# Token rows scattered into slot order in the image loop, and plain loads of 128 rows per expert tile

## What is computed

```python
def reference(x, ...):
    h = tokens(x)                        # (16, 256, 192)
    h = h + attention(layernorm(h))      # 12 heads of 16, then a layernorm with gain and bias
    h = h + ffn(layernorm(h))
    return h

def ffn(x):
    probs = softmax(x @ Wr.T)            # 16 experts
    top_p, top_idx = top_k(probs, 2)
    for e in range(16):
        y += gate[e] * (gelu(x @ W1[e] + b1[e]) @ W2[e] + b2[e])   # gate is 0 where e isn't chosen
    return x + y
```

## Time and profile before

| | us |
|---|---|
| median of 3 runs | 898.73 (895.57 to 900.16) |
| profiled execution, its time | 903.53 |
| its span, first to last instruction | 901.7 |
| TensorE busy (matmul) | 741.2 (82%) |
| VectorE, ScalarE, GpSimd busy | 362.6, 355.0, 432.4 |
| mean granted TensorE clock | 0.907 of 2.4 GHz |

### The profile page before, as it was taken

One profiled execution on the slowest core, in us unless ns is written; L12 is line 12 of the kernel. 1 busy time (PEld: TensorE's weight loads), 2 busy tenths in 40 slices (PEclk: granted clock), 3 DMA queues, 4 the chain that ended last, 5 costly groups with the idle time before them and its releaser, 6 DMA issues.

```text
span 901.7 us, 18009 instructions
## 1 busy us (share of the span) xinstructions
PE 741.2 (82%) x5773; PEld 625.9 (69%) x5773; DVE 362.6 (40%) x984; ACT 355.0 (39%) x857; POOL 432.4 (48%) x618
## 2 busy tenths in 40 slices
PE   0776899967998989897842599999999999999950
PEld 0664567755776766675531499999999999999950
DVE  3101567844676857685453111111111111111128
ACT  0222376643565756564410133333333333333310
POOL 6751234644666756675674244444444443444310
PEclk9995699987999999998855699999999999999985
DMA  7614455576566576664101693726598777686239
GB/s 192 119 43 87 90 116 115 95 93 69 82 115 90 112 86 113 96 119 69 26 25 39 198 326 96 221 82 194 180 315 276 219 222 226 216 260 196 52 104 333
DMA packets 117477, 128.66 MB, mean 143 GB/s; under 512 B 23911, under 2 KB 102008, under 8 KB 117346
## 3 DMA queue, kind: packets, MB, share of 16 engines
q1 hardware_dynamic: 105906, 106.97, 49.1%
q0 software_dynamic: 11504, 20.85, 7.6%
HBM read 145.45 MB, written 29.89 MB: 194 GB/s over the span
## 4 chain that ended last, share of the span: by engine, by line
PE 69%; DMA 13%; DVE 6%; SPq 5%; issue 3%; ACT 2%; POOL 1%; DVEq 0%; ACTq 0%; POOLq 0%
PE BK L419 17%; PE BK L404 12%; PE BK L409 8%; DMA shared<-qk_parts 6%; PE BK L774 4%; PE BK L689 4%; PE BK L794 4%; PE BK L815 4%; PE BK L394 3%; DMA shared<-nmT 3%; PE BK L854 3%; PE BK L826 2%; DVE hr L525 2%; SPq L614 2%; PE BK L782 2%
## 5 line engine op out<-in xcount | busy, mean ns | idle before, releaser
L440 ACT ACTIVATE pixels<-BK,b1t 128x128 f32<-128x128 f32 x474 | 130.7, 375 | 222.0 <-PE BK L409 222.0
L553 POOL DMA_INDIRECT pair_rows<-shared x79 | 77.7, 983 | 190.4 <-DVE shared L507 186.6
L419 PE MATMUL BK<-shared,pixels 128*128 128x192 f32 x948 | 167.9, 326 | 0.3 <-ACT pixels L440 0.3
L419 PEld LDWEIGHTS BK<-shared,pixels 128*128 128x128 f32 x948 | 153.0, 190 | 0.7 <-ACT pixels L440 0.6
L1227 DVE TENSOR_REDUCE negmax<-BK 128x6 f32<-128x1536 f32 x64 | 112.5, 1758 | 34.9 <-PE BK L794 33.6
L404 PE MATMUL BK<-shared 128*128 128x128 f32 x948 | 120.0, 277 | 0.0
L404 PEld LDWEIGHTS BK<-shared 128*128 128x128 f32 x948 | 117.0, 193 | 0.5 <-DVE shared L499 0.3
L1053 ACT ACTIVATE shared<-BK 128x1536 f32<-128x1536 f32 x64 | 92.7, 1449 | 39.5 <-PE BK L815 35.2
L499 DVE COPY shared<-BK 128x256 f32<-128x256 f32 x79 | 33.6, 425 | 181.4 <-PE BK L394 181.4
L547 POOL DMA_INDIRECT shared<-x_rows,shared x79 | 76.0, 962 | 32.6 <-issue 23.2
L1454 POOL DMA_INDIRECT slot_ids<-vid,adr x64 | 64.7, 1010 | 36.3 <-issue 13.4
(11 more groups left out here) (179 smaller groups left out, 1000.6 us busy)
## 6 DMA issues: line engine op xcount, KB each, us to landing
shared<-ew SPq DMA_DIRECT2D x79, 576.0 KB
shared<-ew SPq DMA_DIRECT2D x79, 384.0 KB
shared<-up_rest SPq DMA_DIRECT2D x79, 192.0 KB
shared<-qk_parts SPq DMA_DIRECT2D x112, 96.0 KB
shared<-eb SPq DMA_DIRECT2D x79, 96.0 KB
qk_parts<-shared SPq DMA_DIRECT2D x32, 192.0 KB, 2.1
shared<-qk_parts SPq DMA_DIRECT2D x16, 288.0 KB
qk_parts<-shared SPq DMA_DIRECT2D x32, 96.0 KB, 2.4
```

What stands on the lines that cost most here:

```text
L419: last = nc.tensor.matmul(Y[p], hT[p][:, c * P:(c + 1) * P], w2b[w][:, c, :], start=(c == 0), stop=(c == FC - 1))
L440: last = nc.scalar.activation(hT[p][:, c * P:(c + 1) * P], H[p][c], ACT.Gelu, bias=b1t[:, c, t:t + 1])
L553: nc.gpsimd.indirect_dma_start(pair_d, bass.IndirectOffsetOnAxis(t_dst[:, t:t + 1], 0), ysum[t % NB][:, :], None).then_inc(s[f"m_sc{t % NB ...
```

## The change

`x2_d` and the table `id_d` are gone. One DRAM tensor `slot_d` holds, for each expert, 128 rows of padding (`PR` = 16 rows per partition or block) and then its slots in order, and 2048 more padding rows at the end. A row has 208 numbers (832 bytes): 192 of the token row, then the pair's number, then 15 unused. ScalarE copies each normalized row twice, once per choice, into `xr` (two buffers by parity), GpSimd adds the step to the numbers in place, and its four scatters per image write whole rows of 832 bytes by the same addresses (ranks now begin at 128, because the counts start from 1 on each partition). `b_xc` waits for the scatters of the image two before; `b_vid` waits for `b_xc`. SyncE's two stores per image go.

Before its loop, GpSimd fills the padding rows: 2048 rows in front of the experts' segments, then, after changing the numbers in the source tile, the 2048 rows at the end; it waits for each.

In the routing, VectorE computes for tile t its expert, its first row in `slot_d`, and how many of its rows the tile before has already (the last tile of an expert ends at the expert's last row, so it may overlap; rows that come twice, and padding, get target rows of their own through `offm`). Three diagonal matrices and one matmul with ones bring the three lists into one row. The gather of slot numbers and its transpose go.

In the expert loop SyncE loads 128 consecutive rows for tile t+1 between `first(t)` and `second(t-1)`, with a `value_load` of the first row; GpSimd's gather goes. The second transpose has 64 columns instead of 128; VectorE copies the transpose in three pieces, the last two into both halves of the partitions, and adds `t_dst` per tile. The wait for all image-loop scatters now stands in SyncE, ahead of the first weights. The loads in the tail go to `pair0` instead of `xrow`.

```diff
-    x2_d = nc.dram_tensor("x2_rows", ((NT + 1) * P, 2 * P), fp32).ap()
+    slot_d = nc.dram_tensor("slot_rows", (NE * SEG + P * PR, RW), fp32).ap()
...
         def moe_loads(sp):
             sp.wait_ge(s["r_tab"], 1)
             sp.wait_ge(s["st_w1c"], 32 * NE)
+            for p in range(2):
+                sp.wait_ge(s[f"st_id{p}"], 16 * TOPK * TT * B // 2 + 16)
+
+            def rows(t):
+                at = sp.value_load(rowi[0:1, t:t + 1], min_val=0, max_val=NE * SEG + P * PR - P)
+                wait_prev(sp, s["m_xT"], t - NB + 1)
+                sp.dma_start(xt[t % NB][:, :], slot_d[ds(at, P), :]).then_inc(s[f"m_x{t % NB}"], 16)
...
             before = chosen(0)
+            rows(0)
             first(0, *before)
+            rows(1)
             for t in range(1, NTILE):
                 now = chosen(t)
                 first(t, *now)
+                if t + 1 < NTILE:
+                    rows(t + 1)
                 second(t - 1, *before)
...
+            pe.wait_ge(s["r_diagd"], 3)
+            nc.tensor.matmul(BK[:, 0, 0:3 * P], ones[:, :], r_diag[:, :, :].rearrange("p k t -> p (k t)"),
+                             start=True, stop=True).then_inc(s["pe_row"], 1)
...
-                for c in range(2):
-                    last = nc.tensor.matmul(XT[p][:, c * P:(c + 1) * P], xt[r][:, c * P:(c + 1) * P],
-                                            ident[:, :], start=True, stop=True, is_transpose=True)
-                last.then_inc(s["m_tr"], 1)
+                nc.tensor.matmul(XT[p][:, 0:P], xt[r][:, 0:P], ident[:, :], start=True, stop=True, is_transpose=True)
+                nc.tensor.matmul(XT[p][0:KR, P:2 * P], xt[r][:, P:E], ident[:, :],
+                                 start=True, stop=True, is_transpose=True).then_inc(s["m_tr"], 1)
...
             def rows_T(t):
                 p = t % 2
                 dve.wait_ge(s["m_tr"], t + 1)
+                V.tensor_tensor(t_dst[:, t:t + 1], xt[t % NB][:, E:E + 1], offm[:, t:t + 1], ALU.add)
                 wait_prev(dve, s["m_s1"], t - 1)
-                V.tensor_copy(xtT[p][:, :, :], XT[p][:, 0:2 * P].rearrange("p (c t) -> p c t", c=2)) \
-                    .then_inc(s["m_xT"], 1)
+                V.tensor_copy(xtT[p][:, 0, :], XT[p][:, 0:P])
+                V.tensor_copy(xtT[p][0:KR, 1, :], XT[p][0:KR, P:2 * P])
+                V.tensor_copy(xtT[p][KR:P, 1, :], XT[p][0:KR, P:2 * P]).then_inc(s["m_xT"], 1)
...
-            def rows(t):
-                if t >= NB:
-                    pool.wait_ge(s["m_tr"], t - NB + 1)
-                nc.gpsimd.indirect_dma_start(xt[t % NB][:, :], None, x2_d,
-                                             bass.IndirectOffsetOnAxis(t_src[:, t:t + 1], 0)) \
-                    .then_inc(s[f"m_x{t % NB}"], 16)
...
-            def st_rows(j):
-                apart(sp)
-                sp.wait_ge(s["act_xc"], j + 1)
-                rows = x2_d[0:NTOK, :].rearrange("(p t) e -> p t e", t=NT)[:, ds(TT * j, TT), :]
-                sp.dma_start(rows[:, :, 0:E], xrow[:, ds(TT * j, TT), :]).then_inc(s["st_x2"], 16)
-                sp.dma_start(rows[:, :, E:2 * P], xrow[:, ds(TT * j, TT), P:E]).then_inc(s["st_x2"], 16)
...
-            def b_xc(j):
+            def b_xc(j, p):
+                act.wait_ge(s[f"st_id{p}"], 16 * TOPK * TT * half(j, p) + 16)
                 act.wait_ge(s["dve_x2"], j + 1)
-                nc.scalar.activation(xrow[:, ds(TT * j, TT), :], x2c[:, :, :], ACT.Copy).then_inc(s["act_xc"], 1)
+                nc.scalar.activation(xr[p][:, :, :, 0:E], x2c[:, :, :].unsqueeze(2).to_broadcast([P, TT, TOPK, E]), ACT.Copy) \
+                    .then_inc(s["act_xc"], 1)
...
+            nc.vector.memset(padt[:, :, :], 0.0)
+            for p in range(2):
+                nc.vector.memset(xr[p][:, :, :, :], 0.0)
...
-            nc.gpsimd.dma_start(zeros[:, 0:2 * P], padrow[:, :]).then_inc(s["st_id0"], 16)
-            nc.gpsimd.dma_start(zeros[:, 2 * P:4 * P], padrow[:, :]).then_inc(s["st_id1"], 16)
-            nc.gpsimd.dma_start(zeros[:, 4 * P:ROWS], padrow[:, 0:ROWS - 4 * P]).then_inc(s["ld_zero"], 16)
-            pool.wait_ge(s["ld_zero"], 16)
+            nc.gpsimd.dma_start(slot_d[0:NE * SEG, :].rearrange("(e s) c -> e s c", e=NE)[:, 0:P, :]
+                                .rearrange("e (b r) c -> e b (r c)", r=PR),
+                                padt[:, :, :].rearrange("p r c -> p (r c)")).then_inc(s["st_id0"], 16)
+            pool.wait_ge(s["st_id0"], 16)
+            nc.gpsimd.tensor_copy(padt[:, :, E], pad_v[:, 1, :]).then_inc(s["pool_pad"], 1)
+            pool.wait_ge(s["pool_pad"], 1)
+            nc.gpsimd.dma_start(slot_d[NE * SEG:NE * SEG + P * PR, :].rearrange("(p r) c -> p (r c)", r=PR),
+                                padt[:, :, :].rearrange("p r c -> p (r c)")).then_inc(s["st_id1"], 16)
             for p in range(2):
                 pool.wait_ge(s[f"st_id{p}"], 16)
...
-                nc.gpsimd.indirect_dma_start(id_d, bass.IndirectOffsetOnAxis(adr[p][:, k, t:t + 1], 0),
-                                             vid[p][:, k, t:t + 1], None).then_inc(s[f"st_id{p}"], 16)
+                nc.gpsimd.indirect_dma_start(slot_d, bass.IndirectOffsetOnAxis(adr[p][:, k, t:t + 1], 0),
+                                             xr[p][:, t, k, :], None).then_inc(s[f"st_id{p}"], 16)
```

More of the change, by code:

```diff
@@ L208, in vit_tower @@
         var3 = sb("var3", [P, TT])
-        xrow = sb("xrow", [P, NT, E])
+        xr = [sb(f"xr{p}", [P, TT, TOPK, RW]) for p in range(2)]
+        padt = sb("padt", [P, PR, RW])
+        pad_v = sb("pad_v", [P, 2, PR])
         x2T = sb("x2T", [KH, 2 * T])
@@ L212, in vit_tower @@
         cum = sb("cum", [P, 2, TT, NE], bf16)
-        vid = [sb(f"vid{p}", [P, TOPK, TT]) for p in range(2)]
         adr = [sb(f"adr{p}", [P, TOPK, TT], i32) for p in range(2)]
         x2c = sb("x2c", [P, TT, E])
-        padrow = sb("padrow", [P, 2 * P])
         b1r = sb("b1r", [NE, FF])
@@ L231, in vit_tower @@
         r_ti = late([P, NE], i32)
-        r_tn = late([P, NE])
         r_te = [late([P, NE]) for k in range(2)]
@@ L253, in vit_tower @@
         NB = 4
-        xt = [late([P, 2 * P]) for b in range(NB)]
-        r_df = late([P, NTILE])
-        r_of = late([P, NTILE])
-        t_src = late([P, NTILE], i32)
+        xt = [late([P, RW]) for b in range(NB)]
         t_dst = late([P, NTILE], i32)
@@ L364, in moe_loads @@
                 at = slice(c * CT, (c + 1) * CT)
-                for dst, row in ((xrow, 0), (pair1, FIRST)):
+                for dst, row in ((pair0, 0), (pair1, FIRST)):
                     sp.dma_start(dst[:, at, :], pair_d[row:row + NTOK, :].rearrange("(p t) e -> p t e", t=NT)[:, at, :]) \
@@ L487, in moe_vector @@
-            then(V.tensor_tensor(r_of[:, :], r_df[:, :], r_of[:, :], ALU.subtract))
-            V.tensor_scalar(t_src[:, :], r_of[:, :], float(NTOK), None, ALU.min).then_inc(s["r_meta"], 1)
-            V.tensor_copy(t_dst[:, :], r_df[:, :]).then_inc(s["r_meta"], 1)
+            V.tensor_tensor(r_st[:, :], r_le[:, :], ends[:, :], ALU.mult)
+            then(V.tensor_reduce(r_e[:, :], r_le[:, :], AX.X, ALU.add))
+            V.tensor_reduce(r_s[:, :], r_st[:, :], AX.X, ALU.max)
+            then(V.tensor_scalar(r_oh[:, :], iota[:, 0:NE + 1], r_e[:, 0:1], None, ALU.is_equal))
@@ new lines, in moe_vector @@
+            V.tensor_tensor(r_x4[:, 0:1], pid[:, :], r_s[:, :], ALU.subtract)
+            then(V.tensor_tensor(r_oh[:, :], r_oh[:, :], tot[:, :], ALU.mult))
+            V.tensor_scalar(r_x4[:, 1:2], r_x4[:, 0:1], float(P), float(P), ALU.mult, ALU.add)
+            then(V.tensor_reduce(r_t[:, :], r_oh[:, :], AX.X, ALU.add))
+            then(V.tensor_tensor(r_t[:, :], r_t[:, :], r_x4[:, 1:2], ALU.min))
+            V.tensor_tensor(r_x4[:, 2:3], r_x4[:, 1:2], r_t[:, :], ALU.subtract)
+            V.scalar_tensor_tensor(r_x4[:, 3:4], r_e[:, :], float(SEG), r_t[:, :], ALU.mult, ALU.add)
@@ new lines, in moe_vector @@
+            then(V.tensor_scalar(r_e[:, :], r_e[:, :], float(NE - 1), None, ALU.min))
+            V.tensor_scalar(r_diag[:, 0, :], ident[:, :], r_e[:, 0:1], None, ALU.mult).then_inc(s["r_diagd"], 1)
+            V.tensor_scalar(r_diag[:, 1, :], ident[:, :], r_x4[:, 3:4], None, ALU.mult).then_inc(s["r_diagd"], 1)
+            V.tensor_scalar(r_diag[:, 2, :], ident[:, :], r_x4[:, 2:3], None, ALU.mult).then_inc(s["r_diagd"], 1)
+            dve.wait_ge(s["pe_row"], 1)
+            r_tf, r_at, r_dup = (BK[:, 0, k * P:k * P + NTILE] for k in range(3))
@@ L522, in moe_vector @@
                 dve.wait_ge(s[f"ld_p{c}"], 32)
-                for k, rows in ((0, xrow), (1, pair1)):
+                for k, rows in ((0, pair0), (1, pair1)):
                     for t in range(c * CT, (c + 1) * CT):
@@ L554, in place @@
                                              ysum[t % NB][:, :], None).then_inc(s[f"m_sc{t % NB}"], 16)
-            for t in range(NB):
-                rows(t)
             for t in range(NTILE):
```

(13 more changed lines are left out.)

101 lines of the change are left out of this document (37 added, 64 removed).

## The result

The kernel after takes 858.53 us (median of 4 runs, 856.60 to 862.82) against 897.15 us for the kernel before on the same chip (4 runs, 894.42 to 900.16). The ratio is 0.9575, its 95% interval 0.9524 to 0.9627. Predicted were 856 us, 845 to 880. The profiled run of the kernel after took 857.63 us, its span 855.8; the one of before had a span of 901.7.

What follows compares the result with a forecast made beforehand. The prediction took TensorE as the main bound, with about 41 us lost to a stall from 4-byte scatters. Image loop -36, start +7.5 and routing -14.5 sum to -43.0, from 898.73 to 856 us; range 845 to 880.

Steps and rivals of the forecast that it cites:

- Image loop, forecast -36: Image loop: 832-byte scatters end the stall, ten images go from 231.4 to 195 us; ends -41 and 0.
- no K load to disturb: Image loop, later images: without K loads there, the changed scatters were to gain nothing.
- The cause: Image loop: 4-byte scattered rows write slowly and hold up what shares their engines; about 41 us lost.
- The rival that the stall is not of the 4-byte rows: Image loop: issuing scatters at all, or the K loads, cause the stall; -36 becomes 0, 892 us; chance 0.14.
- Start, forecast +7.5: Before GpSimd's loop: two bare fills of 7.0 us each delay image 0; ends +5.4 and +11.2.
- Routing, forecast -14.5: Last scatter to first up matmul: two of three transfers go, 508.21 becomes 493.9; ends -10 and -16.5.
- Expert loop, forecast 0: Expert loop: TensorE stays the bound at 4.537 us per tile; SyncE's added load fits, so 0.
- no slack to speak of: Expert loop: SyncE needs 4.54 us per tile with new weights, against TensorE's 4.537.
- The rival that SyncE becomes the bound: Expert loop: the added load costs 1.6 instead of 1.15 us, +13, 869 us; chance 0.10.
- The slower rival: Image loop: big scatters stall the Q/K loads by their bytes, +52 over ten images, 944 us; chance 0.06.
- twice at most: Image loop: ScalarE's copy, 0.517 us, at most doubles, +0.5 us per image, counted as nothing because covered.

## Why the prediction was right, step by step

*Image loop, forecast -36, measured -38.7.* The reading that images of 23.1 us would fall to about 19.5 held in size: 20.0. It missed two terms of opposite sign, 5 us too much and 7.2 too little, and that they nearly cancel is luck. (a) The last microsecond: I took image 3 as the floor and priced the scatters by their transfer (0.5 us). What the scatters move costs nothing; the four of them cost 1.1 us per image all the same (18.9 without them). In the trace of before that was hidden under the stall, since no image with scatters and without stall stood there; 10 x 0.5 us of gain too much. (b) The stretch behind the ten images was put at nothing ("no K load to disturb"), and gave -7.2. What differs is the granted clock (1.00 is 2.4 GHz, 0.50 is 1.2, a figure between is a mean of both): before it was at 0.81 from 406.65 to 425.00 and 0.83 in the 20 us after; in the kernel after it is 1.00 until 421, and TensorE's busy time of the stretch is 41.3 instead of 46.3 us. Windows of before, then of after (columns as above):

```profile
406.65:425.00 18.35, 13.24 (x101) 9.40 (x99) 9.46 (x29) 7.33 (x11) 9.11 (x17) 0.81 0.39 73
425.00:445.00 20.00, 17.31 (x141) 12.22 (x144) 12.79 (x41) 10.59 (x16) 13.92 (x24) 0.83 0.12 29
```

```profile
383.08:401.00 17.92, 15.30 (x143) 10.80 (x141) 14.32 (x36) 10.42 (x16) 13.02 (x23) 1.00 0.36 89
401.00:421.00 20.00, 14.85 (x152) 9.44 (x150) 11.07 (x39) 10.59 (x16) 13.90 (x22) 1.00 0.09 30
```

That the stalls bring this low clock with them is not shown. The kernel that stores its rows late has the stall (230.0 us for ten images), and its clock is 1.00 for the 18 us behind them, the stretch 72.1 us; the kernel with 416-byte rows has no stall, and its stretch is 72.0; the one with the extra register load has none either, and takes 75.1. So part of the -7.2 may be chance of the two profiled runs.

*The cause, wrong as it was put.* "The 4-byte rows are slow to write and hold up what shares their engines" failed: 4-byte rows 832 or 16 bytes apart hold up nothing, and 8 bytes apart they leave the length of the images alone. The step that failed is the inference from two rows that differ in more than one thing: the scatters of the earlier trace rows and those of the earlier trace rows differ in size and in whether neighbours touch, and I named the size. The rival that the stall is not of the 4-byte rows had 0.14, but none of its two forms (issuing scatters, the K loads) was the truth either. The forecast held since the change removed both, the small size and the close neighbours: for this step that was luck. The rule of the Trainium skill that I weighed there (page "DMA: Bandwidth & Descriptors", section Specifications: below 512 B, the smallest transfer for full rate, the DMA does a read-modify-write) says nothing of neighbours. No run here shows a price of the size: rows of 4, 64 and 416 bytes give the images of 832.

*Start, forecast +7.5, measured +7.9.* The sum held (its own terms give 73.3 - 66.00 = 7.3, and in the same way 5.1 where it says +5.3), the split did not: the fills took 9.4 and 5.8 us, not twice 7.0. That the two errors cancel is luck. The first one is issued right behind the last gathers, the second with nothing of GpSimd's ahead of it; the two also write to different places, and which of the two makes the 3.6 us no run tells. The estimate of 5.9 us per fill by the Trainium skill (page "DMA: Bandwidth & Descriptors", section "Anatomy of one DMA", SWDGE path) fits the second and not the first. That the old zero stores were covered and the new fills bare was right, and the version with SyncE's fills gives the 7.8 us back.

*Routing, forecast -14.5, measured -15.1.* The first rows were issued at 456.59, 4.0 us behind the last scatter's issue instead of 5.5: the scatter is seen landed after 2.35 us and not 3.9, which is still the wait that ends last, and SyncE's 1.65 us from there are the 1.6 of the sum. From the first rows it took 5.8 us to the first up matmul instead of 5.0. The term, -15.1, lies inside its ends.

*Expert loop, forecast 0, measured -0.1.* That there is "no slack to speak of" held: 4.64 us from tile to tile where SyncE lags (forecast 4.54), hidden only by tiles without new weights, and half a microsecond more costs 27 us. The rival that SyncE becomes the bound was nearer than its 0.10 looked.

*The slower rival*, scatters that stall loads by their bytes, is refuted by the windows with 4 and 832 bytes, which are alike. ScalarE's copy takes 0.84 us (0.517 before), within its "twice at most"; whether it or VectorE's and GpSimd's order makes the 0.3 us between the images of the kernel after (20.0) and those with slots 8 bytes apart (19.7) was not tried.

## What to carry to other kernels

When a transfer looks slow, write down every way in which it differs from the fast one beside it, and change one at a time before building on it: here a distance of 8 instead of 4 bytes between small rows gave the span (854.6 us) that the rewrite gave (855.8). A rewrite that removes a stall should be compared with the smallest edit that removes it, because its own costs (fills on the path, instructions on a busy engine) stay hidden behind the stall's gain. And where a stretch with unchanged code changes its length, look at its granted clock, and at several runs of it, before booking the difference to the change.

## What the runs showed of the hardware

- Scatters of 4-byte rows into slots 4 bytes apart held up other queues' loads: images of 23.1 us against 19.6 to 19.7 with slots 8, 16, 20 or 64 bytes apart. At 8 bytes the six K loads still took 5.13 us of SyncE's queue, against 3.6 to 4.3 from 16 bytes on and 8.17 at 4. Stores of others landed late as well: the copy into `up_rest` took 8.6 us to land in the image from 175.3 us of the kernel before, and 2.4 in the one from 183.2 of the kernel after. The same kernel took 897 and 884 us on different chips while images without the stall repeat to 0.1 us, so the stall may not cost the same everywhere; no profile shows it. How it comes about no row shows either. The row size alone (4 to 832 bytes, 832 bytes apart) changed nothing.
- A scatter costs its engine the same 1.0 us whether it moves 512 bytes or 106 KB, and lands in 2.1 to 5.1 us either way where its rows are 832 bytes apart.
- The same small operation of VectorE took 0.17 us or 0.92 us, and where the timelines were read the long ones lie beside GpSimd's operations of 1.0 us. Moving one scatter on GpSimd lengthened the images from 20.0 to 20.6 us; that it did so through VectorE is read from that, not tested.
- Two transfers of 1.70 MB from GpSimd took 9.4 us right behind gathers and 5.8 us alone; issued by SyncE beside other work they took 9.9 and 11.9 us.
